# One attention half of v turned by VectorE in 32-row blocks, narrow products in another order, and the last output tile stored in two parts

## The reference

```python
# x: (8, 128, 512)
w = quantize(cond_W + lora_delta) + lora_delta       # 8 levels, scale per 128 channels
a = x @ w.T
q, k, v = split(a @ Wqkv + bqkv, 3)                  # 128 channels each
attn = softmax(q @ k.T / sqrt(128))                  # within each sequence of 128
x = x + (attn @ v) @ Wo + bo

base = x @ W2.T
gates = top-2 softmax over 8 experts of (x @ Wr.T + language bias)
y2 = base + 2 * sum over experts of gate[e] * (x @ A[e].T) @ B[e].T
x = x + y2 @ (scale * (qweight - zero_point)).T + bias
```

## Time and profile before

| what | value |
|---|---|
| median of 3 runs | 107.92 us (107.66 to 108.25) |
| profiled execution, its own time | 108.04 us |
| span of its profile | 106.2 us |
| PE busy | 101.5 us (96%), 505 matmuls |
| DVE busy | 66.3 us (62%), 157 instructions |
| ACT busy | 51.9 us (49%), 92 instructions |
| POOL busy | 34.3 us (32%), 34 instructions |
| granted TensorE clock, mean | 0.997 |

### The profile page before, as it was taken

How to read it: one execution, slowest core, us unless ns; L and a number is a source line. 1 busy time by engine, 2 the same in 40 slices (tenths; PEclk the granted TensorE clock), 3 DMA queues, 4 the chain that set the end, 5 groups by cost and what they waited for, 6 DMA issues and landing times.

```text
span 106.2 us, 1428 instructions
## 1 busy us (share of the span) xinstructions
PE 101.5 (96%) x505; PEld 83.6 (79%) x505; DVE 66.3 (62%) x157; ACT 51.9 (49%) x92; POOL 34.3 (32%) x34
## 2 busy tenths in 40 slices
PE   6899999999999999999999999999999999999980
PEld 6734588889777899899888787889898888888850
DVE  1196799999999899325999653014946802572440
ACT  4038789999999954734222238272038204002000
POOL 3000063799919993696000056400000400000000
PEclk9999999999999999999999999999999999999998
DMA  1999999960000000000000000000000540000072
GB/s 38 323 259 396 408 402 406 408 244 0 3 0 0 0 0 0 9 0 0 0 0 0 0 0 0 0 6 0 0 0 0 225 170 0 6 0 0 0 294 104
DMA packets 4455, 9.83 MB, mean 93 GB/s; under 512 B 736, under 2 KB 736, under 8 KB 4448
## 3 DMA queue, kind: packets, MB, share of 16 engines
q1 hardware_dynamic: 4304, 9.48, 24.3%
q10 hardware_dynamic: 144, 0.26, 0.8%
HBM read 7.64 MB, written 2.10 MB: 92 GB/s over the span
## 4 chain that ended last, share of the span: by engine, by line
PE 89%; DMA 4%; DVE 3%; ACT 1%; issue 0%
PE psum L860 19%; PE psum L862 19%; PE psum L861 19%; PE psum L884 7%; PE psum L876 4%; DMA lora<-in_lora 4%; PE psum L895 3%; PE psum L910 3%; PE psum L901 3%; PE psum L905 3%; PE psum L1011 2%; PE psum L1032 2%; PE psum L1026 2%; ACT moe L459 1%; PE psum L1018 1%; PE psum L928 1%
## 5 line engine op out<-in xcount | busy, mean ns | idle before, releaser
L665 DVE COPY_PREDICATED cond_work<-cond_work,psum 128x1024 f32<-128x1024 int32 x10 | 13.7, 1374 | 1.3 <-ACT cond_work L359 0.9
L860 PE MATMUL psum<-G_hi,xT_hi 128*128 128x512 f32 x32 | 12.9, 402 | 0.0
L861 PE MATMUL psum<-G_lo,xT_hi 128*128 128x512 f32 x32 | 12.5, 391 | 0.0
L862 PE MATMUL psum<-G_hi,xT_lo 128*128 128x512 f32 x32 | 12.5, 390 | 0.0
L578 POOL TENSOR_TENSOR hl<-hl,hl_bias 128x272 f32<-128x272 f32 (+2 forms) x4 | 3.1, 774 | 27.0 <-ACT hl L370 14.3
L359 ACT ACTIVATE cond_work<-cond_n,cut_bias 128x1024 f32<-128x1024 f32 x10 | 11.4, 1158 | 0.7 <-DVE cond_n L704 0.7
L520 POOL TENSOR_TENSOR xT_lo<-xT,xT_hi 128x1024 fp32r<-128x1024 f32 x4 | 9.6, 2402 | 2.4 <-DVE cond_work L671 2.4
L860 PE MATMUL psum<-xT_hi,split_b_hi 128*128 128x512 f32 x24 | 9.7, 402 | 0.0
L862 PE MATMUL psum<-xT_hi,split_b_lo 128*128 128x512 f32 x24 | 9.4, 391 | 0.0
L861 PE MATMUL psum<-xT_lo,split_b_hi 128*128 128x512 f32 x24 | 9.4, 390 | 0.0
L520 POOL TENSOR_TENSOR split_a_lo<-moe,split_a_hi 128x512 fp32r<-128x512 f32 x3 | 4.3, 1436 | 15.0 <-ACT split_a_hi L336 12.5
(11 more groups left out here) (168 smaller groups left out, 239.8 us busy)
## 6 DMA issues: line engine op xcount, KB each, us to landing
out<-cond_work SPq DMA_DIRECT2D x8, 256.0 KB, 2.1
q_i<-in_q_t SPq DMA_DIRECT2D x4, 256.0 KB, 7.5
moe<-in_moe_w SPq DMA_DIRECT2D x4, 256.0 KB, 7.5
cond_n<-in_cond_w SPq DMA_DIRECT2D x2, 512.0 KB, 7.1
xT<-in_x_t SPq DMA_DIRECT2D x2, 512.0 KB, 8.2
xT<-in_x_t SPq DMA_DIRECT2D x1, 1024.0 KB, 12.7
wqkv_n<-in_wqkv SPq DMA_DIRECT2D x1, 768.0 KB, 10.7
hlT<-in_hl_t SPq DMA_DIRECT2D x1, 272.0 KB, 6.7
```

Source lines behind the costliest of these rows:

```text
L665: dve.copy_predicated(by_group(half(level, h)), by_group(beyond[n % len(beyond)].bitcast(I32)), psum[EARLY][:, at:at + GROUPS // 2].unsque ...
L860: pe.matmul(out_ap, l_hi, r_hi, start=first, stop=False)
L861: pe.matmul(out_ap, l_hi, r_lo, start=False, stop=False)
L862: return pe.matmul(out_ap, l_lo, r_hi, start=False, stop=last)
```

## The change

It has three parts.

1. **v of the second half.** `v_rows(1, 2)` on TensorE and `v_out(1, 2)` on ScalarE are gone. A new helper `v_turn` on VectorE turns v instead: each 128x128 block is cut into 4x4 squares of 32x32, and one instruction reads 32 partitions and 4x32 columns (the same square of all four sequences) and writes it to its turned place. That makes 16 instructions. Twelve stand behind `softmax_norm(0)` and ahead of `o_lo(0)`; four stand behind `softmax_max(1)` and ahead of `gh_lo(0)`. `attend(1)` waits for a new semaphore that counts these 16. The first half is turned as before.
2. **Order of narrow products.** On TensorE `y_o(0)` (three 512-column products) moves ahead of `scores(1)`.
3. **The last tile.** The bias addition of tile 7 is done in two halves of 256 columns, and SyncE sends each half when it is there, 128 KB each. The final wait counts one store more.

```diff
@@ SyncE
-            for b in range(BATCH):
+            for b in range(BATCH - 1):
                 sp.wait_ge(y_ready, b + 1)
                 sp.dma_start(out[b], y_out[:, b, :]).then_inc(stored, 16)
-            sp.wait_ge(stored, 16 * BATCH)
+            b = BATCH - 1
+            for n in range(2):
+                sp.wait_ge(y_ready, b + n + 1)
+                s = slice(n * C // 2, (n + 1) * C // 2)
+                sp.dma_start(out[b, :, s], y_out[:, b, s]).then_inc(stored, 16)
+            sp.wait_ge(stored, 16 * (BATCH + 1))
...
+        def v_quads(ap, n):
+            return ap[:, 1, :].rearrange("p (b n) -> p b n", b=TPH)[:, :, n * QUAD:(n + 1) * QUAD]
@@ ScalarE
             exps(1, 0)
-            v_out(1, 2)
             hl_raw(3, 3)
@@ VectorE
+            def v_turn(columns):
+                dve.wait_ge(qkvT_ready, 4)
+                for k in columns:
+                    for d in range(QUADS):
+                        dve.transpose(v_quads(v, d)[k * QUAD:(k + 1) * QUAD], v_quads(vT, k)[d * QUAD:(d + 1) * QUAD])\
+                           .then_inc(v_late_ready, 1)
...
-            def y_store(t):
+            def y_store(t, n=slice(0, C)):
                 dve.wait_ge(y_done, t + 1)
                 dve.wait_ge(y_bias_ready, 1)
-                dve.tensor_tensor(y_out[:, t, :], psum[4 + t % 4][:, :], y_bias[:, :], ALU.add).then_inc(y_ready, 1)
+                dve.tensor_tensor(y_out[:, t, n], psum[4 + t % 4][:, n], y_bias[:, n], ALU.add).then_inc(y_ready, 1)
...
             softmax_norm(0)
+            v_turn(range(0, 3))
             o_lo(0)
             gating(0, (1, 2))
             softmax_max(1, 0)
+            v_turn(range(3, QUADS))
             gh_lo(0, 1)
...
-            for t in range(TPH, BATCH):
+            for t in range(TPH, BATCH - 1):
                 y_store(t)
+            for n in range(2):
+                y_store(BATCH - 1, slice(n * C // 2, (n + 1) * C // 2))
@@ TensorE
-                pe.wait_ge(v_ready, h + 1)
+                if h == 0:
+                    pe.wait_ge(v_ready, 1)
+                else:
+                    pe.wait_ge(v_late_ready, QUADS * QUADS)
...
             o_hl(0, 1, 2)
+            pe.wait_ge(oT_hi_ready, 1)
+            pe.wait_ge(oT_lo_ready, 1)
+            y_o(0)
             pe.wait_ge(qkvT_ready, 6)
             scores(1, 0)
-            pe.wait_ge(oT_hi_ready, 1)
-            pe.wait_ge(oT_lo_ready, 1)
-            for t in range(TPH):
+            for t in range(1, TPH):
                 y_o(t)
             x_hl(3, 3, (5,))
             gh_turn(0, 1)
             x_hl(3, 3, (6, 7))
-            v_rows(1, 2)
             pe.wait_ge(ghT_hi_ready, 1)
```

More of the change, by code:

```diff
@@ L61, in block_kernel @@
     SOFTMAX_SCALE = float(D) ** -0.5
+    QUAD = 32
+    QUADS = P // QUAD
     LORA_COPIES = 2
@@ L254, in block_kernel @@
         max_ready = sem("max_ready")
+        v_late_ready = sem("v_late_ready")
         probs_ready = sem("probs_ready")
```

## The result

The changed kernel takes 107.38 us (median of 14 runs, 106.48 to 107.71), the kernel before 107.98 (14 runs). The ratio is 0.9931, with a 95% interval of 0.9915 to 0.9948: 0.5 to 0.9% faster. The forecast was 107.2 us, 0.73 us less than before.

A forecast was written before the change was run, and what follows sets the result against it. TensorE's unbroken row of matmuls was taken as the bound. Turns -0.44, order -0.12 and split store -0.17 sum to -0.73 us, from the median 107.92 to 107.2 us, range 106.85 to 107.9.

The forecast's parts named there:

- The limit for the second place: VectorE ahead of gh_lo(0): the four turns there stay free up to 0.40 us each.
- no idle time ahead of `gh_lo(0)`: Sign on VectorE's timeline that the prediction is wrong; it expected four turns to end at 79.0, gh_lo(0) before at 79.44.
- the wait for q: TensorE's second-half scores wait for ScalarE's copy of q; moving y_o(0) ahead removes this, -0.12 us.
- a price of the pair of narrow groups: Rival at TensorE's scores: two narrow groups in a row cost the 0.12 us, not q; 107.3 us, chance 0.08.
- the straight line: Last store: line through 160 ns for 4 KB and 91 for 2 KB rows, giving 57 ns for 1 KB.
- its data can begin at 104.65: Last tile's second half, issued at 103.90 once the first issue is over; the first half's data begin at 104.32.
- the last data 0.7 us behind the first at the latest: Sign at the last tile's store: last data end within 0.7 us of the first half's data start.
- 2 us and 436 GB/s: Skill page's fixed part and byte rate of one DMA; by it 128 KB less in the last store saves 0.30 us.
- the split store gives nothing: Rival at the last tile's store: 1 KB pieces cost as much as 2 KB ones; 107.9 us, chance 0.12.
- 0.54 + 0.06 + 0.03: Chance of a measurably faster kernel, below 107.38 us: most of forecast, last rival, part of the second; given as about 0.61.
- The slow rival: VectorE's turns cost 0.69 us each, stalling TensorE 2.4 us in all; 109.6 us, decides from 0.40 us, chance 0.07.

The follow-up runs named there:

- e1: Kernel before with only the turning of v moved to VectorE, old product order and one whole last store: 107.52 us, ratio 0.9954.
- e6: Changed kernel with four more turns, written to an unused place, behind the four ahead of gh_lo(0): 108.63 us, ratio 1.0077.
- e2: Kernel before with only y_o(0) moved ahead of the second half's scores, v still turned by TensorE: 107.89 us, ratio 0.9984.
- e4: Changed kernel with the last tile stored whole, keeping the turning on VectorE and the new order: 107.35 us, ratio 0.9947.
- e7: Changed kernel with the second part of the last tile's store issued from ScalarE's queue instead of SyncE's: 107.25 us, ratio 0.9946.
- e11: Changed kernel with the second half of the last tile not sent at all: 106.73 us, ratio 0.9894.
- e3: Kernel before with only the last tile added and stored in two parts: 107.85 us, ratio 0.9984.
- e5: Changed kernel with all 16 turns ahead of o_lo(0) and none ahead of gh_lo(0): 107.23 us, ratio 0.9957.
- e10: Changed kernel run again without any edit, beside the others on the same chip: 107.31 us, ratio 0.9937.
- e8: Changed kernel with TensorE's wait ahead of the first half's turned probabilities filled by the first block of qkv(1, 1): 107.02 us, ratio 0.9925.

## Why the prediction was right, step by step

**Part 1, the turns: right, with less room than forecast.** Forecast -0.44 us; e1 gives 0.45 on the chain. A turn takes 0.302 us, taken was 0.28, and the next one starts 0.33 to 0.34 us behind it (1.32 us for four; 5.30 for sixteen), so they don't overlap, as assumed. The limit for the second place was forecast as 0.40 us for each turn, with 0.06 us for the signal. By e6 the signal takes 0.14 us and 0.11 us were free, so the limit is 0.33 + 0.11 / 4 = 0.36 us. The mechanism is as forecast, but that 0.33 us stayed below it is a narrow margin and in part luck.

The prediction named as a sign that it is wrong: no idle time ahead of `gh_lo(0)`. That came true, since the four turns end at 79.13 instead of 79.0, just when ScalarE's matrix is ready. The sign was the wrong one: `gh_lo` loses nothing by that, and `y_gh` isn't late. The one to watch is the time between `gh_lo`'s end and `y_gh`.

The Trainium skill, "VectorE: DVE Perf Modes", "The three transpose paths", gives 311 ns in bf16, close to the 302 ns for 128 f32 elements on 32 partitions here. The Trainium skill's rule in "Two Vector instructions with no wait between them" on the same page, that a new start group of partitions holds an instruction, agrees with turns of 0.30 us that start every 0.33 us; no run here had turns without such a change, so the cause isn't shown.

**Part 2, the order: right.** Forecast -0.12; e2 gives 0.14, e4 against e1 0.17 on TensorE's part. That the new order takes the 0.12 us away, and that nothing else grows, is shown by e2. That they were the wait for q and not a price of the pair of narrow groups rests on rows (the weight loads shown under e2) and on no run of its own.

**Part 3, the store: the mechanism was there, the size wasn't.** Forecast -0.17; the profiles give about -0.05. The sum had the first data 0.28 us sooner behind TensorE (1.49 to 1.21) and the data 0.11 us longer (0.8 to 0.91). Measured is 0.26 us sooner (1.57 to 1.31), the data 0.19 us longer (0.82 to 1.01) and what follows 0.03 us longer. The time from issue to data was read 0.08 us too short (0.75 instead of 0.83), but in both kernels, so this cancels.

The price of small rows was right in kind and a little high: a packet of 2 KB takes 84 ns and one of 1 KB 46 ns, where the straight line had 91 and 57. The step that failed is "its data can begin at 104.65", 0.33 us behind the first half's, so that they follow without a pause. Measured is 0.48 us (103.68 and 104.16): the second issue began 0.38 us behind the first and took 0.43 us instead of 0.33. A half keeps an engine busy for 0.37 us only, so each engine stood idle for about 0.1 us between the halves. The small rows cost the rest, about 0.1 us: 0.76 us of engine time for both halves (0.4 x 0.87 + 0.10 x 0.39 + 0.4 x 0.87 + 0.10 x 0.21) against 0.67 for the whole tile (0.7 x 0.87 + 0.1 x 0.54 + 0.01).

e7 takes the pause away and gets 0.1 us back. e11 shows that the last byte is what counts. The prediction's text also asks for the last data 0.7 us behind the first at the latest, while its own sum has 0.91.

The prediction's 2 us and 436 GB/s stand in the Trainium skill, "DMA: Bandwidth & Descriptors", for transfers that GpSimd issues; this store is issued by SyncE, so that its 2.1 us to landing don't test them. The sum didn't use them.

**The sum.** -0.44 - 0.12 - 0.17 = -0.73 was forecast. The profiles give -0.63 for TensorE's part and -0.05 for the end, -0.68 together; the medians give -0.60, and the interval of the ratio is -0.56 to -0.92 us. The sum came nearer than its terms: the store gave 0.12 us less than forecast, TensorE's part 0.07 more than 0.56, of which about 0.03 is scatter (e3, which changes nothing there, has 0.03 as well). Of the 0.18 us between 107.2 and 107.38, 0.06 are the kernel before itself, whose median was 107.92 in three runs and 107.98 in fourteen. The rival "the split store gives nothing" named the right term, but neither its time (107.9) nor its reason came true: a 1 KB piece doesn't cost as much as 2 KB. One addition is off: 0.54 + 0.06 + 0.03 is 0.63 and not 0.61.

**The slow rival** was to decide from 0.40 us on. e6 shows its mechanism with twice the number of turns in the second place: a late `gh_lo` comes through to the end almost whole.

## What to carry to other kernels

Where one engine's instructions form the whole chain, price a change by what each piece adds to that chain, and compare equal shapes in it: the group that adds more than its twin (scores 1.01 against 0.89, turned probabilities 0.66 against 0.44) hides a wait, and other work moved ahead of it wins the difference. Work moved to an idle engine is free only up to the next wait in that engine's list; the nearest such wait, not the total idle time, is the limit. Splitting the last store gives little here when both issues stand in one queue (0.05 us) and more when the second comes from another engine's (0.14 us): the second issue and the smaller rows eat most of the head start.

## What the runs showed that was not expected

- The first half of the kernel scatters more than all that was changed. Up to the first half's scores, which no variant touches, the profiles take 59.68 us (e7) to 60.69 (e5), e10's 62.03 left aside. The first eight matmuls of the kernel last 4.57 us before and 3.79 after:

```profile
4.81 4.57 PE L876 MATMUL psum<-lora 128*128 128x512 f32 x8 [0.40 <-DMA lora<-in_lora]
```
```profile
4.67 3.79 PE L897 MATMUL psum<-lora 128*128 128x512 f32 x8 [0.26 <-DMA lora<-in_lora]
```

The window views read a granted clock of 1.00 there in both, but the trace's record of the clock begins only at 6.61 us before and at 4.93 after; ahead of it nothing is on record. In the kernel before, these matmuls start 0.98 and 0.84 us apart ahead of 6.61 and 0.43 us apart behind it; after, the first two starts are 0.62 us apart and the others 0.43. All the profiles with such a record go the same way: where it begins late, the first eight take long (it begins at 4.23 us in e5 and at 7.05 in e8, and they take 3.67 and 4.75 us). A lower clock ahead of the record would fit the pace; why it begins earlier or later wasn't tried. It isn't the whole of the scatter: of the 0.78 us between before and after, 0.11 are left at the first half's scores, and e5, whose first eight are among the shortest, is the latest there. Because of this scatter differences of 0.1 us were read from parts of the profile and not from times.
- An issue of a store took SyncE 0.33 us alone and 0.43 us when it stood right behind another one; in every profile of two SyncE stores, the pair took 0.81 us.
- From the last data to the end of the span it was 0.73 to 0.78 us in all profiles, whether 256 or 128 KB were sent last.
